# The order of the scan stage's steps: filters end at state 6, decays two states ahead, row sums, D*u and the gate's silu elsewhere

## What is computed

```
xz = einsum('bld,ed->bel', layernorm(x), W_in);  x, z = halves of xz          # 256 channels each
x1, x2 = silu(causal conv of x, 4 taps, dilation 1), silu(the same, dilation 2)
xc = gate[0] * x1 + gate[1] * x2
dt_low, B, C = split(W_x @ xc, 64, 16, 16)
delta = softplus(W_dt @ dt_low + b_dt);  A = -exp(A_log)
for each token t:                                  # 16 states n for each channel
    h[n] = h[n] * exp(delta_t * A[n]) + delta_t * B_t[n] * x_t
    y_t  = sum over n of h[n] * C_t[n]
out = W_out @ ((y + D * xc) * silu(z))
```

## Time and profile before

| | us |
|---|---|
| median of 3 runs | 3467.05 (3467.03 to 3468.33) |
| the profiled execution | 3465.32 |
| its span in the profile | 3463.5 |
| scan stage in it, first scan to end of the last | 1818.0 to 3072.7 |

### The profile page before, as it was taken

One profiled execution on the slowest core, in us unless ns is written; L12 is line 12 of the kernel. 1 busy time (PEld: TensorE's weight loads), 2 busy tenths in 40 slices (PEclk: granted clock), 3 DMA queues, 4 the chain that ended last, 5 costly groups with the idle time before them and its releaser, 6 DMA issues. The chain is left out here.

```text
span 3463.5 us, 50385 instructions
## 1 busy us (share of the span) xinstructions
PE 2444.5 (71%) x12608; PEld 1746.5 (50%) x12608; DVE 2279.3 (66%) x6241; ACT 1532.4 (44%) x2928; POOL 1684.0 (49%) x1350
## 2 busy tenths in 40 slices
PE   2409995666399943199937888777777778738992
PEld 2309994555389933199913333333333333318992
DVE  3604445666544468155528999999999999974553
ACT  0005554444255511055535555565555555524551
POOL 1755551333345537455504565655555566654551
PEclk9999997788699965599968889888888889879996
DMA  8127871111178732278723333333333333317776
GB/s 260 54 80 230 226 213 51 39 47 37 38 230 227 227 104 78 87 229 227 205 86 105 117 124 124 112 129 110 120 126 122 110 122 116 117 52 217 226 229 178
DMA packets 262510, 478.93 MB, mean 138 GB/s; under 512 B 37309, under 2 KB 173467, under 8 KB 262272
## 3 DMA queue, kind: packets, MB, share of 16 engines
q1 hardware_dynamic: 202576, 388.64, 37.9%
q0 software_dynamic: 34816, 68.00, 5.5%
q10 hardware_dynamic: 25008, 21.11, 1.9%
HBM read 383.22 MB, written 98.54 MB: 139 GB/s over the span
## 5 line engine op out<-in xcount | busy, mean ns | idle before, releaser
L1420 POOL TENSOR_TENSOR ssm_HC<-ssm_H,ssm_BC 128x1024 f32<-128x1024 f32 x256 | 601.4, 2349 | 590.6 <-DVE ssm_psX L1482 541.8
L1243 PE MATMUL ssm_psY<-ssm_HC,ident 128*128 128x512 f32 x1024 | 554.7, 673 | 201.8 <-POOL ssm_HC L1420 201.2
L1488 DVE TENSOR_TENSOR_SCAN ssm_H<-ssm_dA,ssm_psX 128x1024 f32<-128x1024 f32 x256 | 585.3, 2286 | 45.1 <-issue 32.0
L1243 PEld LDWEIGHTS ssm_psY<-ssm_HC,ident 128*128 128x128 f32 x1024 | 205.1, 210 | 499.9 <-POOL ssm_HC L1420 272.4
L1352 ACT ACTIVATE ssm_dA<-ssm_delta,ssm_A 128x511 f32<-128x511 f32 x512 | 329.7, 708 | 102.5 <-DVE ssm_delta L1457 100.0
L374 POOL DMA_INDIRECT xslots<-att_r_xn,att_r_idx x128 | 127.1, 993 | 284.3 <-DVE att_r_idx L351 248.3
L1205 PE MATMUL ssm_psA<-ssm_hT,ssm_Wtap 128*128 128x512 f32 x512 | 245.1, 614 | 2.5 <-ACT ssm_hT L1304 2.5
L709 POOL DMA_INDIRECT d_back<-d_yr,d_to_row x144 | 139.8, 971 | 155.4 <-DVE d_yr L784 131.7
L709 POOL DMA_INDIRECT c_back<-c_yr,c_to_row x144 | 139.8, 971 | 155.1 <-DVE c_yr L784 133.1
L709 POOL DMA_INDIRECT b_back<-b_yr,b_to_row x144 | 139.8, 971 | 154.5 <-DVE b_yr L784 132.6
L709 POOL DMA_INDIRECT a_back<-a_yr,a_to_row x144 | 139.8, 971 | 154.0 <-DVE a_yr L784 132.0
(11 more groups left out here) (513 smaller groups left out, 5724.7 us busy)
## 6 DMA issues: line engine op xcount, KB each, us to landing
ssm_BC<-bc_rows SPq DMA_DIRECT2D x128, 1024.0 KB
a_W<-in_l_pack SPq DMA_DIRECT2D x72, 514.0 KB
b_W<-in_l_pack SPq DMA_DIRECT2D x72, 514.0 KB
c_W<-in_l_pack SPq DMA_DIRECT2D x72, 514.0 KB
d_W<-in_l_pack SPq DMA_DIRECT2D x72, 514.0 KB
a_xs<-xslots SPq DMA_DIRECT2D x72, 131.0 KB
b_xs<-xslots SPq DMA_DIRECT2D x72, 131.0 KB
c_xs<-xslots SPq DMA_DIRECT2D x72, 131.0 KB
```

The lines of the kernel that those rows point to most:

```text
L1243: last = nc.tensor.matmul(psY[:, dt, :], k.ident[:, :], HC[:, n % RP, (dt + n) % DT, :], start=False, stop=(n == NB - 1))
L1420: nc.gpsimd.tensor_tensor(HC[:, n % RP, :, :], H[:, n % RH, :, :], BC[:, n // CHUNK % SLOTS, 1, n % CHUNK:n % CHUNK + 1, :].to_broadcast([ ...
L1488: nc.vector.tensor_tensor_scan(flat(H[:, n % RH, :, :]), flat(dA[:, n % RA, :, :]), flat(psX[:, odd:odd + DT, :]), 0.0, ALU.mult, ALU.add) ...
```

## The change

In the scan stage alone, only the order is changed:

- filters: the taps of the four filters end in step 5 and the gate's two filters stand in step 6 (before: 7); they are emptied in steps 3 to 6 and 8
- ScalarE's decays run two states ahead (before: one)
- the silu of the filters stands in step 6 (before: 8), in a block with the silu of the gate z of the current sequence, which before was done a sequence earlier; `act_0` goes to 7, `act_1` to 9, `to_low` to 9, `soften` from 13 to 10, `act_2` from 10 to 11
- VectorE: `mix` from 10 to 8, `dve_2b` from 12 to 11, `step_sizes_1` from 14 to 12, `step_sizes_2` from 15 to 13; statistics of s + 2 in step 0 (before: 6), `normalize` in 4 (before: 9)
- TensorE: `project` from 10 to 8, `steps` from 12 to 9, `pe_1b` from 9 to 10, `pe_2` from 13 to 12, `flip` from 15 to 13; the row sums of s + 3 in step 15, where those of s + 2 stood in step 4; D*u with state 9 (step 11)
- ahead of the first sequence the first silu comes before the gate's filters are emptied, and the row sums of sequence 2 are made there

```diff
@@ -1081,9 +1081,9 @@
...
-CONV_STEPS = {1: ((0, (0, 1)),), 2: ((0, (2, 3)),), 3: ((1, (0, 1, 2)),), 4: ((1, (3,)), (2, (0, 1))), 5: ((2, (2, 3)), (3, (0,))),
-              6: ((3, (1, 2, 3)),), 7: ((4, (0,)), (5, (0,)))}
-EMPTY_STEPS = {2: (0,), 4: (1,), 5: (2,), 7: (3,), 8: (4, 5)}
+CONV_STEPS = {1: ((0, (0, 1, 2)),), 2: ((0, (3,)), (1, (0, 1))), 3: ((1, (2, 3)), (2, (0,))), 4: ((2, (1, 2, 3)),), 5: ((3, (0, 1, 2, 3)),),
+              6: ((4, (0,)), (5, (0,)))}
+EMPTY_STEPS = {3: (0,), 4: (1,), 5: (2,), 6: (3,), 8: (4, 5)}
...
@@ -1112,6 +1112,7 @@
...
         ST, NB = SEQ_TILES, STATES
+        SKIP = 9
         CHUNK, SLOTS = 2, 4
...
@@ -1234,13 +1235,13 @@
...
                 pe.wait_ge(hc_ready, s * NB + n + 1)
-                if n == 0:
-                    if positive(s):
-                        pe.wait_ge(y_ready, s)
+                if n == 0 and positive(s):
+                    pe.wait_ge(y_ready, s)
+                if n == SKIP:
                     for dt in range(DT):
-                        nc.tensor.matmul(psY[:, dt, :], diag[:, dt, :], xc[:, b, dt, :], start=True, stop=False)
+                        nc.tensor.matmul(psY[:, dt, :], diag[:, dt, :], xc[:, b, dt, :], start=False, stop=False)
                 for dt in range(DT):
-                    last = nc.tensor.matmul(psY[:, dt, :], k.ident[:, :], HC[:, n % RP, (dt + n) % DT, :], start=False, stop=(n == NB - 1))
+                    last = nc.tensor.matmul(psY[:, dt, :], k.ident[:, :], HC[:, n % RP, (dt + n) % DT, :], start=(n == 0), stop=(n == NB - 1))
                 last.then_inc(y_summed, 1)
...
@@ -1256,28 +1257,28 @@
...
                     if n == 7:
-                        if there(s, 2):
-                            pe.wait_ge(G.taken, s + 3)
+                        pe.wait_ge(added, s)
                         R.pe_1a(nc, pe, s - 1, 1 - b)
-                    if n == 9:
+                    if n == 10:
                         R.pe_1b(nc, pe, s - 1, 1 - b)
-                    if n == 13:
+                    if n == 12:
                         R.pe_2(nc, pe, s - 1, 1 - b)
...
                         conv(s + 1, g, taps)
-                    if n == 10:
+                    if n == 8:
                         project(s + 1, 1 - b)
-                    if n == 12:
+                    if n == 9:
                         steps(s + 1)
                 if there(s, 2):
-                    if n == 4:
+                    if n == 13:
+                        flip(s + 2)
+                if there(s, 3):
+                    if n == 15:
                         if there(s, -1):
-                            pe.wait_ge(added, s)
-                        G.pe(nc, pe, s + 2, b, turn + 1, psR4)
-                    if n == 15:
-                        flip(s + 2)
+                            pe.wait_ge(R.rowed, s)
+                        G.pe(nc, pe, s + 3, 1 - b, turn + 1 + b, psR4)
...
@@ -1288,6 +1289,7 @@
...
             flip(1)
+            G.pe(nc, pe, 2, 0, 1, psR4)
             run(pe, main, between)
...
@@ -1312,11 +1314,18 @@
...
             def silu(s, b):
                 act.preload_act_table_set("silu_and_others")
+                if there(s, 1):
+                    act.wait_ge(emptied, s * 6 + 10)
+                    nc.scalar.activation(pre[:, :, :], pre[:, :, :], ACT.Silu).then_inc(silu_done, 1)
                 act.wait_ge(emptied, s * 6 + 6)
-                nc.scalar.activation(pre[:, :, :], pre[:, :, :], ACT.Silu).then_inc(silu_done, 1)
                 nc.scalar.activation(zs[:, b, :, :], zs[:, b, :, :], ACT.Silu).then_inc(z_done, 1)
                 act.preload_act_table_set("natural_log_exp_and_others")
+                if there(s, 1):
+                    half(s + 1, 1 - b)
+            def half(s, b):
                 act.wait_ge(silu_done, s + 1)
...
@@ -1353,36 +1362,37 @@
...
             def main(s, b, n):
-                if n + 1 < NB:
-                    decay(s, b, n + 1)
+                if n + 2 < NB:
+                    decay(s, b, n + 2)
                 elif there(s, 1):
-                    decay(s + 1, 1 - b, 0)
+                    decay(s + 1, 1 - b, n + 2 - NB)
             def between(s, b, turn, n):
-                if there(s, -1):
-                    if n == 4:
-                        R.norm.act_root(nc, act, s - 1)
-                    if n == 6:
-                        R.act_0(nc, act, s - 1, 1 - b, turn - 1 + b)
-                    if n == 8:
-                        R.act_1(nc, act, s - 1, 1 - b)
-                    if n == 10:
-                        R.act_2(nc, act, s - 1)
                 if there(s, 1):
...
                         to_hT(s + 1)
-                    if n == 7 and there(s, 2):
+                    if n == 9:
+                        to_low(s + 1)
+                if there(s, -1):
+                    if n == 4:
+                        R.norm.act_root(nc, act, s - 1)
+                    if n == 7:
+                        R.act_0(nc, act, s - 1, 1 - b, turn - 1 + b)
+                    if n == 9:
+                        R.act_1(nc, act, s - 1, 1 - b)
+                    if n == 11:
+                        R.act_2(nc, act, s - 1)
+                if n == 6:
+                    silu(s, b)
+                if there(s, 1) and n == 10:
+                    soften(s + 1)
+                if there(s, 2):
+                    if n == 2:
                         N.act_root(nc, act, s + 2)
-                    if n == 8:
-                        silu(s + 1, 1 - b)
-                    if n == 11:
-                        to_low(s + 1)
-                    if n == 13:
-                        soften(s + 1)
-                if there(s, 2):
-                    if n == 11:
+                    if n == 5:
                         N.act_apply(nc, act, xn, s + 2).then_inc(normed, 1)
...
@@ -1393,14 +1403,21 @@
...
             to_hT(0)
-            for g in range(6):
+            for g in range(4):
                 empty(0, 0, g)
-            silu(0, 0)
+            act.preload_act_table_set("silu_and_others")
+            act.wait_ge(emptied, 4)
+            nc.scalar.activation(pre[:, :, :], pre[:, :, :], ACT.Silu).then_inc(silu_done, 1)
+            act.preload_act_table_set("natural_log_exp_and_others")
+            half(0, 0)
+            for g in range(4, 6):
+                empty(0, 0, g)
             to_low(0)
...
             decay(0, 0, 0)
+            decay(0, 0, 1)
             run(act, main, between)
...
@@ -1499,21 +1516,21 @@
...
                         R.dve_2a(nc, dve, chain, s - 1, 1 - b)
-                    if n == 12:
+                    if n == 11:
                         R.dve_2b(nc, dve, chain, s - 1, 1 - b)
...
                 if there(s, 1):
-                    if n == 10:
+                    if n == 8:
                         mix(s + 1, 1 - b)
-                    if n == 14:
+                    if n == 12:
                         step_sizes_1(s + 1, 1 - b)
-                    if n == 15:
+                    if n == 13:
                         step_sizes_2(s + 1, 1 - b)
                 if there(s, 2):
-                    if n == 6:
+                    if n == 0:
                         stats(s + 2, b, turn + 1)
-                    if n == 9:
+                    if n == 4:
                         normalize(s + 2)
...
```

More of the change, by code:

```diff
@@ L1472, in main @@
             def main(s, b, n):
+                c = n // CHUNK
                 if n == 0:
                     dve.wait_ge(ux_ready, s + 1)
-                c = n // CHUNK
                 if n % CHUNK == 0:
```

## The result

| | before | after |
|---|---|---|
| median, us | 3467.69 (3467.03 to 3468.78, 4 runs) | 3538.81 (3535.30 to 3539.16, 4 runs) |
| span of the profiled execution | 3463.5 | 3536.8 |
| first scan to start of the last | 1252.4 | 1326.9 |

The changed kernel takes 1.0202 times as long, with an interval of 1.0185 to 1.0220: 71 us more. It is slower well beyond the noise; whether by more than 2% is left open by the interval. Forecast were 3514 (49 more than the profiled execution of the kernel before) and a range of 3490 to 3540.

The account below looks back on a forecast made before the run. The prediction took VectorE to bound the scan stage. From the profiled execution's 3465.3 us it took off 37.0 of gains and added 86 of new waits, giving 3514, with a range of 3490 to 3540.

Parts of the forecast that it names:

- What bounds the kernel: Scan stage: VectorE is the bound, with waits of only 32.0 and 4.8 us in a stretch of 1255 us.
- The scan's waits: VectorE's waits ahead of the scan, mostly state 10, go with decays two ahead: -30.3 us of 32.0.
- The gate's 4.8 us: VectorE's waits at the gate for a sequence's last sum go, as step sizes move to step 13: -4.8 us.
- the prologue: Ahead of the first scan: the mix starts 2.9 us sooner, 1 us is lost at a row sum, together -1.9.
- The 1.0 us at the first row sum: After its first scan VectorE waits for sequence 2's row sum, now ahead of the first filters: some 1 us.
- What costs nothing: Moved D*u, row sums, row loads and chunks add no wait: priced at 0, with 0 to 2 us for the last sequence.
- The loss: VectorE waits at dve_2b for the exponential, now behind the softening: 6.15 us in 14 sequences, +86 (74 to 101).
- the start of TensorE's chain: TensorE's sum of state 0 starts when GpSimd's product is ready, t = 10.1; filters then run without a break to 30.0.
- The floor of 3483: Rival: mix at 42.5, not filters or ScalarE's queue, delays the projection; wait 3.95 us a sequence, 3483; chance 0.07.
- the unchanged 3428: Rival: the softening is through before VectorE asks at dve_2b, only the -37.0 is left, 3428; chance 0.06.
- table loads of twice the length (3586): Rival: four table loads on the chain each hold ScalarE twice 1.28 us, +72 in 14 sequences, 3586; chance 0.01.
- TensorE slow throughout (3578): Rival: projection, sum of state 7 and step matmuls all at half clock, wait 10.7 us, +150, 3578; chance 0.02.

Follow-up runs that it names:

- e1: Kernel before with only the decays two states ahead: 3543.9 against 3573.0 us, ratio 0.9919; first to last scan 1221.5, 30.9 less.
- e2: Changed kernel with the router's exponential (act_2) back in ScalarE's step 10, ahead of the softening: 3605.4 us; first to last scan 1288.0, 38.9 less.
- e3: Changed kernel with the score matmuls (pe_1b) in TensorE's step 9, ahead of the step matmuls: 3661.7 us; first to last scan 1347.7, 20.8 more.
- e4: Changed kernel with dve_2b in step 12, pe_2 in 13, softening in ScalarE's 12 behind the exponential: 3548.8 us, ratio to kernel before 0.9925.
- e5: The order of e4 with the score matmuls (pe_1b) also in TensorE's step 9: 3528.5 against 3577.4 us, ratio to kernel before 0.9870.
- e8: Changed kernel with the statistics in VectorE's step 1, ahead of the gate, instead of 0: 3649.2 us; first to last scan 1328.2, no change.
- e7: Changed kernel with statistics in VectorE's step 2 instead of 0, output product and root in step 3: 3616.6 us; first to last scan 1298.8, 28.1 less.
- e9: Changed kernel with three more filter taps in TensorE's step 1, ahead of the sum of state 0: 3615.9 us; first to last scan 1299.2, 27.7 less.
- e10: Changed kernel unchanged, on another chip: 3652.6 us against one run of 3575.8 of the kernel before; first to last scan 1328.9.

## Why the forecast was right, and which term was off

The mechanism was right and the time lies in the range, but near its edge: 3538.8 is beyond the 3502 to 3529 that the sum's own bounds gave, and the measured wait, 7.9 us a sequence, is beyond its 5.3 to 7.2. The range reached to 3540 for a second slow group of matmuls in each sequence. What filled it was mostly something else, so that part is luck.

- **What bounds the kernel.** Right. What TensorE, ScalarE or GpSimd gained or lost showed through VectorE's waits; the exception is the mix, which takes 0.23 us longer (last section).
- **The gains.** The scan's waits went, 30.0 us against 30.3, and e1 shows that decays two ahead do it alone. The gate's 4.8 us went. In the prologue, from the stage's first load of tables to the first scan, 76.0 us became 74.4; the forecast had 2.9 less, of which 1.1 had gone when the first filter was emptied, 32.3 us behind that load and not 31.2. The 1.0 us at the first row sum came as forecast. By these terms the gains are 35.5 us. Against the profiled executions they are 37.8 (111.1 less the 73.3 by which they differ), and 37.0 were forecast; that it is so near is in part chance, as the small waits and VectorE's own time of the balance above were not in the sum.
- **What costs nothing.** Right: no wait on the row sums but the first, none on chunks of B and C, none new for the gate. The last sequence cost nothing either.
- **The loss.** The mechanism was right: the softening ahead of the exponential, VectorE late at `dve_2b` in 14 sequences, part of it seen one step sooner at `dve_2a`. e2 and e3 show it from both sides, and e4 and e5 take it away.
- **The term that was mis-sized** is the start of TensorE's chain. The forecast began it with the product of state 0, at 10.1. But `total` of state 0 waits for `y_ready` too, the gate that frees `psY`: 11.1 to 11.3 in 13 sequences and 8.9 in sequence 14 (e8 against e7). That is 0.9 us on average. And it took "without a break" for full clock: in five sequences of the 14 the sum and the output product run at the lower level, 1.7 us more each, 0.6 on average. These two are nearly all of the 1.6 us by which the block starts late. VectorE arrives 0.3 us sooner than at 53.6 (53.3 on average, 50.6 in sequence 14), and the way from the block to VectorE's resuming is 0.2 us shorter than forecast. Together these make the 1.8 us missed in a sequence, by 14 the 25 us to the measured time. In the same way two looped sequences take 11.4 us more than before (the mean of the loop), not 8.
- **Could it be seen before?** The gate could: the wait for `y_ready` stands in the diff, and the forecast has the gate at 10.0 in another place. The clock in part. The earlier trace rows has slow groups behind 4.37 and 4.87 us of idle, and the forecast used that for the projection. For the shorter idle time that the change opens, the trace of before shows both, in two sums of four matmuls:

```profile
2275.63 3.39 PE L1243 MATMUL ssm_psY<-ssm_HC,ident 128*128 128x512 f32 x4 [2.36 <-POOL ssm_HC L1420]
...
2605.54 1.98 PE L1243 MATMUL ssm_psY<-ssm_HC,ident 128*128 128x512 f32 x4 [3.05 <-POOL ssm_HC L1420]
```

- **Small slips in the sum.** 50.1 + 8.14 + 1.22 + 0.23 is 59.7, not 59.75, which is worth 0.8 us in all. The bound of 51.2 for the softening leaves out that transposes and projection are both slow, 52.0.
- **The rivals.** The floor of 3483, the unchanged 3428, table loads of twice the length (3586) and TensorE slow throughout (3578) are all out. The silu (L1321) starts 1.30 us after the start of its table load, which takes 1.28. The Trainium skill's page "ScalarE: Activation LUTs", section "What ACT_TABLE_LOAD costs", adds a drain of some 1.38 us to each switch; this trace doesn't agree, as neither before nor behind the load is there an idle time for it: the ACTIVATE ahead of it starts at 2177.59 and takes 0.69, and the load starts at 2178.29.

## What to carry to other kernels

Where each engine runs a list written by hand, follow one result through all lists before a step is moved: a long block that is put ahead of a short one makes everybody wait who needs the short one, and the engine that is full pays. Read the list of waits as places and not as causes: the longest one here (69.5 us) could be taken away at a loss, and only together with the one behind it at a gain. Change one thing at a time: three lines of this change bring 31 us, and 111 are lost at two waits behind the places of a few others. And where an experiment takes one limit away, look for the next before its gain is booked: e7 and e9 took different ones and stopped at the same sum.

## What the runs showed of the hardware

TensorE's clock doesn't follow from the length of the idle time alone. In the changed kernel TensorE idles ahead of the sum of state 0 in 13 sequences. In five (1, 2, 3, 4 and 6) the idle time is 2.17 to 2.85 us and the clock falls to its lower level behind it; in the other eight it is 2.70 to 2.87 us and sum and output product run at full clock. In e10, the same kernel on another chip, the five are 1, 4, 10, 12 and 13, with 2.62 to 2.87 us, and there are sequences with 2.63 to 2.88 at full clock. In e9, with 0.3 us of idle at most, none of the 14 is slow. So the idle time goes with the falls, and which sequence has one changes between executions of one kernel. What decides it is left open.

VectorE's mix (L1463) takes 1.51 or 1.52 us in sequences 2 to 14 of the changed kernel, 1.33 in sequence 1, and 1.26 to 1.28 in the kernel before; in all it does the same work. In sequence 1 GpSimd has no rows to send, and its product ends 0.25 us into the mix. In sequence 4 the product ends 0.42 us into it, and the row DMA is issued beside it:

```profile
1929.14 1.33 DVE L1463 SCALAR_TENSOR_TENSOR ssm_xc<-ssm_pre,ssm_gates,ssm_xc 128x1024 f32<-128x1024 f32 x1
...
2185.58 1.51 DVE L1463 SCALAR_TENSOR_TENSOR ssm_xc<-ssm_pre,ssm_gates,ssm_xc 128x1024 f32<-128x1024 f32 x1
...
2186.17 1.81 POOL L374 DMA_INDIRECT xslots<-ssm_r_xn,ssm_r_idx  x1 [0.17 <-issue]
```

That VectorE and GpSimd hinder each other is the likely reason, and no run changes this one thing alone.
